# Second attention of a twelve-stage model: in three of eight groups GpSimd bounds and masks the exponentials, in place of a mask product on TensorE

## The reference, cut to what matters

```
q = split_heads(query @ wq_kernel + wq_bias)      # 16 heads of 16 channels, 256 queries
k = split_heads(key @ wk_kernel + wk_bias)        # 4096 keys
v = split_heads(value @ wv_kernel + wv_bias)
scores = jnp.einsum('bhqd,bhkd->bhqk', q, k) / jnp.sqrt(jnp.float32(HD))
m = mask[:, None, :, :]
scores = jnp.where(m == 0, jnp.float32(-1000000000.0), scores)
attn = jax.nn.softmax(scores, axis=-1)
out = jnp.einsum('bhqk,bhkd->bhqd', attn, v)
```

## Time and profile before

| what | value |
|---|---|
| median of three runs | 1589.32 us (1585.78 to 1593.42) |
| the profiled execution, its own time | 1583.62 us |
| its span, first to last instruction | 1582.4 us |
| TensorE busy over the span | 1462.9 us (92%) |
| VectorE busy | 978.0 us (62%) |
| ScalarE busy | 717.1 us (45%) |
| GpSimd busy | 410.3 us (26%) |
| mean granted TensorE clock | 0.96 of full speed |

### The profile page before, as it was taken

How to read it: one execution, slowest core, us unless ns; L and a number is a source line. 1 busy time by engine, 2 the same in 40 slices (tenths; PEclk the granted TensorE clock), 3 DMA queues, 4 the chain that set the end, 5 groups by cost and what they waited for, 6 DMA issues and landing times. The chain is left out here.

```text
span 1582.4 us, 29922 instructions
## 1 busy us (share of the span) xinstructions
PE 1462.9 (92%) x11296; PEld 846.9 (54%) x11296; DVE 978.0 (62%) x2273; ACT 717.1 (45%) x972; POOL 410.3 (26%) x584
## 2 busy tenths in 40 slices
PE   8999987999999988799999888799999897999997
PEld 3665753555555556255555455345555583555555
DVE  4443446888888744777777224388886236888832
ACT  5134221444444531265665433256767221767662
POOL 4555332656666620101101022011111001011100
PEclk9999996999999998799999989889999997999999
DMA  8888992334446043264551094536667521566700
GB/s 272 267 277 255 284 298 84 62 61 62 61 65 151 2 72 50 51 88 76 78 88 35 12 293 151 146 56 96 91 103 212 85 36 44 87 95 93 158 3 7
DMA packets 131658, 178.23 MB, mean 113 GB/s; under 512 B 14365, under 2 KB 105525, under 8 KB 124342
## 3 DMA queue, kind: packets, MB, share of 16 engines
q1 hardware_dynamic: 117610, 160.90, 48.1%
q10 hardware_dynamic: 13904, 15.41, 3.1%
HBM read 132.44 MB, written 43.78 MB: 111 GB/s over the span
## 5 line engine op out<-in xcount | busy, mean ns | idle before, releaser
L861 ACT ACTIVATE prob_a<-ps 128x1024 f32<-128x1024 f32 x512 | 505.5, 1023 | 305.2 <-PE ps L744 215.9
L874 DVE CUSTOM_DVE_ANT_0 dump_a<-ps,neg_q 128x512 bf16<-128x512 f32 (+1 forms) x485 | 328.6, 717 | 104.0 <-PE ps L727 102.5
L727 PE MATMUL ps<-kop,qop 116*128 116x512 bf16 x1024 | 347.4, 410 | 41.1 <-DMA qop<-qparts 23.4
L878 DVE TENSOR_REDUCE best_a<-ps 128x1 f32<-128x512 f32 (+1 forms) x488 | 312.6, 707 | 72.4 <-PE ps L727 72.3
L741 PE MATMUL ps<-qop,kop 116*128 116x256 bf16 x2048 | 350.8, 275 | 5.5 <-ACT prob_a L861 4.9
L741 PEld LDWEIGHTS ps<-qop,kop 116*128 116x128 bf16 x2048 | 196.0, 100 | 138.0 <-ACT prob_a L861 17.9
L727 PEld LDWEIGHTS ps<-kop,qop 116*128 116x128 bf16 x1024 | 87.2, 100 | 205.8 <-issue 85.1
L744 PE MATMUL ps<-neg_k,identb 128*128 128x512 bf16 x512 | 195.5, 382 | 0.0
L766 PE MATMUL ps<-prob_a,vop_a 128*32 128x256 f32 x3072 | 185.0, 382 | 0.0
L952 POOL CAST mpart_a<-nmax_a 128x2 bf16<-128x2 f32 x64 | 25.4, 396 | 601.3 <-DVE nmax_a L883 601.3
L973 POOL TENSOR_TENSOR used_a<-prob_a,gT 128x1024 f32<-128x1024 f32 x64 | 151.5, 2367 | 87.5 <-DVE used_a L891 67.4
(11 more groups left out here) (310 smaller groups left out, 1363.1 us busy)
## 6 DMA issues: line engine op xcount, KB each, us to landing
kop<-kparts SPq DMA_DIRECT2D x448, 128.0 KB, 5.1
kparts<-kp SPq DMA_DIRECT2D x64, 384.0 KB, 4.5
vals<-vst SPq DMA_DIRECT2D x16, 1024.0 KB, 6.4
vraw<-vals SPq DMA_DIRECT2D x64, 256.0 KB, 6.4
e_w<-in_e_w SPq DMA_DIRECT2D x6, 2048.0 KB, 16.6
z_w<-in_z_w SPq DMA_DIRECT2D x24, 256.0 KB, 7.2
ctxT<-in_ctxT SPq DMA_DIRECT2D x8, 512.0 KB, 8.1
raw<-in_mask ACTq DMA_DIRECT2D x16, 256.0 KB, 5.8
```

Of the source, the lines that this page charges most:

```text
L727: return pe.matmul(out, qop[0:R_ALL, h, t * P:(t + 1) * P], kop[0:R_ALL, h % UNROLL, j * CHUNK:(j + 1) * CHUNK], start=True, stop=True)
L861: act.activation(prob[:, n % NP, :], st_bank(n), ACT.Exp).then_inc(S("exp_done"), 1)
L874: dve.tensor_tensor_reduce(out=dump[:, k % 2, 0:width], in0=bank, in1=c.neg_q[:, t, j * CHUNK:j * CHUNK + width], scale=1.0, scalar=-3.0e3 ...
L878: dve.tensor_reduce(out, bank, AX.X, ALU.max).then_inc(sem, 1)
```

## The change

In layer 1 (`SHIELDED`), groups 1, 4 and 6 of each head leave out their two mask products. ScalarE's exponential of such a group is not masked, so where a masked key scores above the maximum over the seen ones it can be large. GpSimd bounds the 128x1024 tile to at most 1 and multiplies it with a 0/1 mask, both in place in `prob`; the value products of the group wait for that (`shielded`). GpSimd's order in a head is: shield group 1, `split(h + 1)`, shield group 4, `fill(h + 1)`, shield group 6.

The 0/1 mask is made once, in place, in those groups' tiles of `neg_k`. A query that sees no key must keep its uniform row: TensorE sums the mask over the keys (32 products of ones with `neg_k`, in place of 16 filling products), VectorE finds the seeing and the blind queries by a threshold, the queries of blind rows are multiplied by 0, and a row of `qop` (number 116, which the shielded groups' products take in as a 117th) holds -2^100 for blind queries, so that they get in every group score and mask alike. The tile `c.idle`, which the filling products use, is 1 in place of 0.

```
+    SHIELD = (1, 4, 6) if l == SHIELDED else ()
...
+            rows = R_ALL + 1 if g in SHIELD else R_ALL
             for j in range(GROUP):
                 k = g * GROUP + j
-                ins = pe.matmul(st_bank(n)[:, j * NT:(j + 1) * NT], kop[0:R_ALL, h % UNROLL, k * P:(k + 1) * P],
-                                qop[0:R_ALL, h, :], start=(j % 2 == 0), stop=(not by_query and j % 2 == 1))
-                if by_query and j % 2 == 1:
+                added = by_query and g not in SHIELD
+                ins = pe.matmul(st_bank(n)[:, j * NT:(j + 1) * NT], kop[0:rows, h % UNROLL, k * P:(k + 1) * P],
+                                qop[0:rows, h, :], start=(j % 2 == 0), stop=(not added and j % 2 == 1))
+                if added and j % 2 == 1:
                     ins = pe.matmul(st_bank(n)[:, (j - 1) * NT:(j + 1) * NT], c.identb[:, :],
                                     c.neg_k[:, k - 1:k + 1, :], start=False, stop=True)
...
+            elif g in SHIELD:
+                pe.wait_ge(S("shielded"), len(SHIELD) * h + SHIELD.index(g) + 1)
...
+        def find_seen(i, g):
+
+            pool.tensor_scalar(seen(g), seen(g), 0.0, None, ALU.is_equal).then_inc(S("seen_found"), 1)
+            pool.wait_ge(S("seen_found"), 2 * i + 1)
+            pool.tensor_tensor(seen(g), seen(g), asked.blind[:, :].unsqueeze(1).to_broadcast((P, GROUP, NT)), ALU.add)\
+                .then_inc(S("seen_found"), 1)
+
+        def shield(h, g):
+
+            n = NGROUP * h + g
+            pool.wait_ge(S("exp_done"), n + 1)
+            if h == 0 and g == SHIELD[0]:
+                pool.wait_ge(S("seen_found"), 2 * len(SHIELD))
+            pool.tensor_scalar(prob[:, n % NP, :], prob[:, n % NP, :], 1.0, None, ALU.min).then_inc(S("bounded"), 1)
+            pool.wait_ge(S("bounded"), len(SHIELD) * h + SHIELD.index(g) + 1)
+            pool.tensor_tensor(prob[:, n % NP, :], prob[:, n % NP, :], seen(g).rearrange("p k q -> p (k q)"), ALU.mult)\
+                .then_inc(S("shielded"), 1)
...
         for h in range(H):
+            for g in SHIELD[:1]:
+                shield(h, g)
             if h + 1 < H:
                 split(h + 1)
+            for g in SHIELD[1:2]:
+                shield(h, g)
...
+            for g in SHIELD[2:]:
+                shield(h, g)
```

In `queries`, the new work of layer 1:

```
+        if l == SHIELDED:
+            dve.wait_ge(S("masks_summed"), 1)
+            limit = (KEYS - 0.5) * NEG
+            dve.tensor_scalar(seeing[:, :], c.ps[:, 7, 0:NT], limit, None, ALU.is_gt).then_inc(S("seeing_found"), 1)
+            dve.tensor_scalar(neg_blind[:, :], c.ps[0:1, 7, 0:NT], limit, NEG, ALU.is_le, ALU.mult)\
+               .then_inc(S("blind_negated"), 1)
+            dve.wait_ge(S("seeing_found"), 1)
+            q.leave_blind_out(dve, S, banks, seeing[:, :], q_all)
+            dve.tensor_scalar(blind[:, :], c.ps[:, 7, 0:NT], limit, None, ALU.is_le).then_inc(S("blind_found"), 1)
+            dve.wait_ge(S("q_seeing"), CT)
+        q.rest_and_third(dve, S, banks, q_all)
...
+        if l == SHIELDED:
+            for k in range(KT):
+                ins = pe.matmul(c.ps[:, 7, 0:NT], c.idle[:, 0:P], c.neg_k[:, k, :], start=(k == 0), stop=(k == KT - 1))
+            ins.then_inc(S("masks_summed"), 1)
```

More of the change, by code:

```diff
@@ L41 @@
 KEYED = 2
+SHIELDED = 1
 NORM_FILL, FOLD_FILL, TOP_FILL = 16, 6, 28
@@ L284, in project, with leave_blind_out, first_and_second @@
             ins.then_inc(S("q_psum"), 1)
-    def first_and_second(self, act, S, banks):
+    def leave_blind_out(self, dve, S, banks, seeing, q):
+        for mt in range(CT):
+            dve.wait_ge(S("q_psum"), mt + 1)
+            dve.scalar_tensor_tensor(out=self.half(q, mt), in0=self.c.ps[:, banks[mt], 0:NT],
+                                     scalar=self.c.bq[:, self.l, mt:mt + 1], in1=seeing, op0=ALU.add, op1=ALU.mult)\
+               .then_inc(S("q_seeing"), 1)
+    def first_and_second(self, act, S, banks, q=None):
         c = self.c
         for mt in range(CT):
-            act.wait_ge(S("q_psum"), mt + 1)
-            act.activation(self.half(self.qp[:, 0, :], mt), c.ps[:, banks[mt], 0:NT], ACT.Identity,
-                           bias=c.bq[:, self.l, mt:mt + 1]).then_inc(S("q_part0"), 1)
+            if q is None:
+                act.wait_ge(S("q_psum"), mt + 1)
+                act.activation(self.half(self.qp[:, 0, :], mt), c.ps[:, banks[mt], 0:NT], ACT.Identity,
+                               bias=c.bq[:, self.l, mt:mt + 1]).then_inc(S("q_part0"), 1)
+            else:
+                act.wait_ge(S("q_seeing"), mt + 1)
+                act.activation(self.half(self.qp[:, 0, :], mt), self.half(q, mt), ACT.Copy).then_inc(S("q_part0"), 1)
         for mt in range(CT):
@@ L295, in first_and_second, with rest_and_third @@
             act.activation(self.half(self.qp[:, 1, :], mt), self.half(self.rest, mt), ACT.Copy).then_inc(S("q_part1"), 1)
[L297 removed]
+    def rest_and_third(self, dve, S, banks, q=None):
         c = self.c
@@ L301, in rest_and_third @@
             dve.wait_ge(S("q_part0"), mt + 1)
+            if q is not None:
+                dve.tensor_tensor(self.half(self.rest, mt), self.half(q, mt), self.half(self.qp[:, 0, :], mt),
+                                  ALU.subtract).then_inc(S("q_rested"), 1)
+                continue
             dve.scalar_tensor_tensor(out=self.half(self.rest, mt), in0=c.ps[:, banks[mt], 0:NT],
@@ L581, in fill_constants @@
 def fill_constants(c, pool, S):
-    for tile, value in ((c.idle, 0.0), (c.fold, 0.0), (c.ones, 1.0), (c.tri, 0.5), (c.den16, 0.0)):
+    for tile, value in ((c.idle, 1.0), (c.fold, 0.0), (c.ones, 1.0), (c.tri, 0.5), (c.den16, 0.0)):
         pool.memset(tile[:, :], value).then_inc(S("later_filled"), 1)
@@ L608, in queries @@
     banks = (1, 2)
+    blind = sb("blind", [P, NT], BF16) if l == SHIELDED else None
+    neg_blind = sb("neg_blind", [1, NT], BF16) if l == SHIELDED else None
     stage = Stage(S)
+    stage.blind = blind
+    seeing = sb("seeing", [P, NT], F32) if l == SHIELDED else None
+    q_all = sb("q_all", [P, CT * NT], F32) if l == SHIELDED else None
     @stage.vector
@@ L634, in _ @@
            .then_inc(S("xT_ready"), 1)
-        q.first_and_second(act, S, banks)
+        q.first_and_second(act, S, banks, q_all)
         q.load_half(act, S, 1)
@@ L646, in _ @@
         q.load_rest(sp)
+        if l == SHIELDED:
+            sp.wait_ge(S("blind_negated"), 1)
+            sp.dma_start(c.qop[R_ALL:R_ALL + 1, :, :], neg_blind[0:1, :].unsqueeze(1).to_broadcast((1, H, NT)))\
+              .then_inc(S("blind_placed"), 16)
     return stage
@@ L982, in _ @@
         fill(0)
+        if l == SHIELDED:
+            pool.wait_ge(asked.S("blind_found"), 1)
+            for i, g in enumerate(SHIELD):
+                find_seen(i, g)
         split(0)
```

7 lines of the change are left out of this document (5 added, 2 removed).

## The result

The changed kernel takes 1622.9 us (median of four runs, 1621.1 to 1626.0) against 1587.8 for the kernel before beside it (four runs, 1585.8 to 1593.4). The ratio on record is 1.0242, 95% interval 1.0218 to 1.0265; the two medians by themselves divide to 1.0221. It is slower by 35 us in the medians and by 38.2 us in the profiled spans (1620.6 against 1582.4). The forecast of 1635 us has the right sign and lies 12 us too high; measured against each side's own base, 46 us were forecast and 35 to 38 came.

A forecast was written before the change was run, and what follows sets the result against it. TensorE's instruction stream was taken to bound the second attention; shielding would make GpSimd the bound, 46 us later at its end. Added to the profiled 1583.6 us this gives 1630, corrected to the runs' median 1635; range 1567 to 1650.

The forecast's parts named there:

- likeliest case: Second attention: GpSimd becomes the bound at 17.3 us a head against TensorE's 13.57; chance 0.60.
- the cover: Start: GpSimd's mask preparation ends at 657.6, before the first split at 658.77 + 0.8, so it costs nothing.
- what sets 1.499 apart is the single operation, and the new one has it: GpSimd's bound priced from a one-operation scaling row of 1.499 us at 512 columns: 2.76 us at 1024.
- the rival's low bound: GpSimd's bound priced from a two-operation row, 0.84 ns a column: 1.12 us at 1024 columns.
- the low price: Rival: GpSimd's bound takes 1.12 us, a head 12.4 us on GpSimd, TensorE still bounds; 18 us faster, 1571; chance 0.28.
- The mask product, taken at 2.37 us: GpSimd's product of exponentials with the 0/1 mask, priced from the form with both inputs f32; 2.26 kept as low end.
- The gaps, taken at 0.13 us a shield: Two gaps between dependent GpSimd instructions in each shielded group, part of its 5.26 us.
- The first shield, taken at 666.9: GpSimd starts shielding after group 1's first exponential: 666.54, less 0.44 for two masks, plus 0.8 for the later start.
- The end, taken at 1.0 us behind GpSimd: After GpSimd ends at 942.0, two value groups (0.93) follow, then ScalarE's last reading of the sums at 943.0.
- The stall at the turn: TensorE waits 3.1 us a head at the turn of the maxima, as the split stands behind shield 1.
- A mask product's 0.22 us: TensorE gains 0.22 us for each removed mask product, 6 a head, 96 in all: 21.1 us.
- The clock: Rival: TensorE's clock falls in the new stalls; half the heads at 1.2 GHz add 78 us, 1713; chance 0.04.

The follow-up runs named there:

- the forms: Fifteen GpSimd instructions on 128x1024 tiles added at the end of the kernel before, each waiting for the last; single operation 2.78 us, multiply/add pair 1.05, pair with minimum 3.63.
- ScalarE's bound and the slot held: Changed kernel with ScalarE bounding as exp(-relu(-s)), score slot kept until the second pass: 1595.9 us with three groups, 1601.1 with two.

## Why the prediction came out as it did

**Right.** The likeliest case was the one that came: GpSimd full from 669 to 931 us (forecast 667 to 942), the bound at 2.765 us for 2.76, TensorE waiting for the split at its turn and, less, at value products, the preparation of the mask hidden (3.8 us left of the cover, 2 forecast), the mask products gone from three groups, no other engine's instructions slower in the heads (VectorE's chunk maxima 0.688 us for 0.689, ScalarE's exponentials 1.022 for 1.023). That the bound, and neither the queue's order nor the start, is the cause is shown: without it, or with a cheap instruction in its place, 1570 and 1573 us; with the split moved ahead, 1624; with no group at all, no change. What it makes full is GpSimd's whole round, so dropping the third group takes the loss away too (1586).

**The step "what sets 1.499 apart is the single operation, and the new one has it"** led to the right figure, and the forms bear it out for the row it was read from, a multiplication: 2.78 us alone, 1.05 as one of a pair. That a second operation would make the bound cheap too does not follow, and is not so: 3.63 us. What the forms show is a price by the operations used. The row of 0.84 ns a column behind the rival's low bound is a fast pair, 1.05 to 1.12 us at this size; a minimum was never seen at that price. That being in place does not count was argued from two rows of two-input sums, of which it is said that one lies on the line of the other; two sizes always make a line, and it is the forms that show it. The rule of the Trainium skill on one-input operations (GPSIMD Engine Reference, section "Engine selection", roughly line rate) was one of the reasons for the low price and its 0.28. The measurement decides: the rule fits the copy (1.036 us) and the pairs (1.05), not one operation (2.78) or a pair with a minimum (3.63). The other half of that rule, two-input operations about half as fast as on VectorE, the prediction called borne out without showing VectorE's row: the same product there (L891 of the kernel before) has a median of 1.220 us, a ratio of 1.9, and a mean of 1.482 us, a ratio of 1.6.

**Terms of the sum, against the traces.** The sum put the last reading of the sums at 943.0 us, and it is at 932.9:

- The mask product, taken at 2.37 us: 2.131 us, 48 x 0.24 = 11.5 us less. The prediction worked out 2.26 for this form and kept it for the low end only, though it was the nearer. Even that was high, as it borrowed the growth by column of the form with two f32 inputs, 2.15 ns; this form grows by (2.131 - 1.155) / 512 = 1.91.
- The gaps, taken at 0.13 us a shield: the rows are 2.85 and 2.07 to 2.10 us apart, 4.94 a shield, where their durations add to 4.90. That is 0.04, so 48 x 0.09 = 4.3 us less (two waits of 1.0 us, in the heads with the lowest clock, give 2.0 back). The row of a product reaches some 0.05 us over the start of the next instruction, which gives back most of the wait behind the bound. A head comes to 3 x 4.94 + 1.53 = 16.3 us, for 17.3.
- The first shield, taken at 666.9: 669.4. The attention begins 0.8 us later in this execution, and its start costs 1.6 us for 0.8. VectorE's chain makes 1.3 of that: its nine instructions take 4.41 us, 0.49 a piece for 0.43. The other 0.3 was not followed. The last 0.9 lie between the first product and the first shield: the sum took 0.44 off for two masks that are gone, but the exponential of group 1 starts 0.35 later instead, counted from the first product. From 665 to 670 us the granted clock is 0.66 here where it was 1.00 before; the bound starts 0.15 after the exponential's end.
- The end, taken at 1.0 us behind GpSimd: 2.1, as the last value products read 1.94 us.

GpSimd's chain so lasts 930.8 - 669.4 = 261.4 us instead of 275.1, 13.7 us less; the start gives 2.5 back and the end 1.1, and 46.0 - 13.7 + 2.5 + 1.1 = 35.9 us, as measured.

**The stall at the turn** was put at 3.1 us a head; it is 1.95 in the mean. The shorter head leaves 16.34 - 13.77 = 2.57 us of stall for 3.8, and of that the heads at 1.00 show 2.4 at the turn; the others show less, as the lower clock takes up the rest. At the value products at most 0.4 us a head came for 0.7, the two last blocks apart. **A mask product's 0.22 us** came to 0.19 with six gone and 0.17 with four. The trace does not name the missing 0.03 to 0.05 us apiece.

**The clock** (0.04) did fall, to 0.77 to 0.97 in many 15 us windows, but not at the price that was put on it. The prediction let a slow head add its whole stretch; GpSimd's pace leaves TensorE 2.5 us a head of slack (16.34 less 13.86), and the slower products went into it, all but 1.0 us in each of two heads: 2 us in all, for 78.

## What to carry to other kernels

Price an elementwise instruction on GpSimd by its operations as well as its shape: two of the same name, size and types lay 3.5 times apart, and no pair with a minimum in it was cheap. When work is moved off a full engine, add up the receiving engine's whole round first; here 3 x 4.9 us stood against a head of 13.8, and a third engine did the bound for 1.06 us. When an engine makes two passes, let the buffer that it reads go after the pass that read it.

## What the runs showed of the hardware

- GpSimd, 128x1024: a single operation 2.77 to 2.79 us, a pair of multiplications or additions 1.04 to 1.05 (1.12 with a scalar from a tile), a pair with minimum 3.63, a copy 1.04. Narrower types did not help: the comparison on bf16 takes 2.77 as on f32.
- A product of f32 by bf16 takes 2.13 us, of f32 by f32 2.36 at the same size.
- ScalarE takes 1.06 us for an exponential of a tile in SBUF, as against 1.01 to 1.02 for one in PSUM, and alternates with Relu (1.02) with no row and no idle time between them.
- In the changed kernel TensorE's granted clock went up and down by heads of 16 to 17 us. After a wait at the turn of 0.2 to 0.8 us the next head had 0.99 to 1.00 (six of six, 707.54 to 889.29). After a wait of 2.2 to 2.4 us it had 0.81 to 0.90 in six heads and 0.99 in one; within such a head the stretch from 840 to 845 us read 0.50, the lower level. With ScalarE's bound and the slot held, where TensorE's rows show no wait over 0.84 us, every 15 us window from 700 to 880 us read 1.00.
